# An adapter and expert FFN kernel on one core: Bx spread by hi/lo products, flips grouped, W's first piece halved, loads and transposes reordered

## The reference, cut to what matters

```python
Bx  = einsum('bni,bri->bnr', x, B[itok])          # x (8, 512, 2048), rank 16
y   = einsum('bnr,bor->bno', Bx, A[itok])
base   = einsum('bsi,oi->bso', y, base_w) + base_b            # base_w (2048, 2048)
hidden = einsum('bsi,ri->bsr', y, ffn_A)                      # rank 64
probs  = softmax(einsum('bsi,ei->bse', y, router_w))          # 16 experts, top 2, renormalised
delta  = einsum('bse,bsr,eor->bso', combine, hidden, ffn_B) * 0.5
out = x + base + delta
```

## Time and profile before

| | us |
|---|---|
| median of 3 runs | 446.18 (445.64 to 464.56) |
| the profiled execution's own time | 445.62 |
| its span, first to last instruction | 443.8 |
| granted TensorE clock, mean | 0.996 |

### The profile page before, as it was taken

How to read it: one execution, slowest core, us unless ns; L and a number is a source line. 1 busy time by engine, 2 the same in 40 slices (tenths; PEclk the granted TensorE clock), 3 DMA queues, 4 the chain that set the end, 5 groups by cost and what they waited for, 6 DMA issues and landing times.

```text
span 443.8 us, 6785 instructions
## 1 busy us (share of the span) xinstructions
PE 409.7 (92%) x2496; PEld 279.9 (63%) x2496; DVE 319.4 (72%) x830; ACT 108.1 (24%) x163; POOL 40.5 (9%) x53
## 2 busy tenths in 40 slices
PE   0597997999788999999999999999999999999996
PEld 0475985656556766666667666666666676666665
DVE  2699996999468496668677875966686778756453
ACT  0003114435473231123113112311231131123110
POOL 4020000002100120012001201200120012012000
PEclk9999998999999999999999999999999999999999
DMA  8999999999999999899999999998999898556935
GB/s 223 357 330 331 334 357 366 345 269 336 289 295 239 352 362 323 279 349 342 310 287 378 306 315 302 366 312 295 348 335 325 285 366 303 207 201 217 343 128 189
DMA packets 75027, 135.35 MB, mean 305 GB/s; under 512 B 5506, under 2 KB 14770, under 8 KB 74994
## 3 DMA queue, kind: packets, MB, share of 16 engines
q1 hardware_dynamic: 56000, 102.08, 69.7%
q10 hardware_dynamic: 18994, 32.84, 23.5%
HBM read 99.23 MB, written 35.65 MB: 304 GB/s over the span
## 4 chain that ended last, share of the span: by engine, by line
PE 63%; DVE 10%; DMA 9%; SPq 6%; POOL 3%; ACT 3%; issue 3%; ACTq 2%; POOLq 0%; DVEq 0%
PE ps L927 13%; PE ps L928 11%; PE ps L929 11%; PE ps L901 11%; PE ps L941 6%; DMA bexpT<-in_x 6%; PE ps L930 5%; POOL u_r L480 3%; DMA gm_r<-xT 3%; DVE xT L728 3%; DVE early L659 3%; SPq L296 3%; ACT bexpT L495 2%; PE ps L856 2%; PE ps L949 2%
## 5 line engine op out<-in xcount | busy, mean ns | idle before, releaser
L840 DVE TENSOR_TENSOR xbuf<-ps,xbuf 128x512 f32<-128x512 f32 x128 | 86.7, 677 | 96.0 <-PE ps L930 96.0
L927 PE MATMUL ps<-h_r,u_r 128*128 128x512 f32 x256 | 108.8, 425 | 0.7
L928 PE MATMUL ps<-h_r,u_r 128*128 128x512 f32 x256 | 100.3, 392 | 0.0
L929 PE MATMUL ps<-h_r,u_r 128*128 128x512 f32 x256 | 100.1, 391 | 0.0
L866 PE MATMUL ps<-early 128*128 128x256 f32 x256 | 66.5, 408 | 22.6 <-DVE early L659 22.6
L728 DVE STREAM_TRANSPOSE xT<-xbuf 128x256 f32<-128x256 f32 x224 | 80.6, 410 | 0.0
L866 PEld LDWEIGHTS ps<-early 128*128 128x128 f32 x256 | 48.1, 201 | 36.8 <-issue 16.5
L927 PEld LDWEIGHTS ps<-h_r,u_r 128*128 128x128 f32 x256 | 48.1, 188 | 35.9 <-issue 16.7
L659 DVE STREAM_TRANSPOSE early<-xbuf 128x256 f32<-128x256 f32 x128 | 65.9, 577 | 5.3 <-issue 3.8
L901 PE MATMUL ps<-bexpT,cur 128*32 128x512 f32 x512 | 61.6, 598 | 2.2 <-DVE h_r L707 1.5
L495 ACT ACTIVATE h_r<-ps 128x512 fp32r<-128x512 f32 x64 | 36.2, 595 | 78.8 <-PE ps L901 78.4
(11 more groups left out here) (67 smaller groups left out, 205.3 us busy)
## 6 DMA issues: line engine op xcount, KB each, us to landing
out<-xbuf SPq DMA_DIRECT2D x31, 1024.0 KB, 7.3
xbuf<-in_x SPq DMA_DIRECT2D x28, 1024.0 KB, 7.4
xbuf<-in_x ACTq DMA_DIRECT2D x32, 512.0 KB, 10.9
xbuf<-in_x SPq DMA_DIRECT2D x32, 512.0 KB, 8.6
xbuf<-in_L_ffn_base_w SPq DMA_DIRECT2D x16, 512.0 KB, 19.3
xbuf<-in_L_ffn_base_w ACTq DMA_DIRECT2D x16, 512.0 KB, 20.1
gm_r<-g_hilo SPq DMA_DIRECT2D x128, 32.0 KB, 6.8
early_u<-in_L_ffn_B SPq DMA_DIRECT2D x10, 256.0 KB, 18.5
```

What stands on the lines that cost most here:

```text
L840: dve.tensor_tensor(xs, ps[:, tile_bank(b.n, m), :], xs, ALU.add).then_inc(s_out, 1)
L927: pe.matmul(acc, u_r[:, b.q, 0, h, tok_t], hi, start=(h == 0), stop=False)
L928: pe.matmul(acc, u_r[:, b.q, 0, h, tok_t], lo, start=False, stop=False)
L929: pe.matmul(acc, u_r[:, b.q, 1, h, tok_t], hi, start=False, stop=False)
```

## The change

- Bx' is split: ACT makes a second copy of the PSUM bank rounded to fp32r (`bxs_r[:, 0]`), DVE subtracts it from `bxp` (`bxs_r[:, 1]`), and PE spreads both by two fp32r products into one sum, in slot 10 (`REP_AT`) instead of 9. ACT's `bx` and `sbx_r` copies move to slot 10 with it.
- Both halves' flips are done in slot 13 (`CT_AT`).
- Bx of batches 2 to 7 starts before tile 4 rather than 3; `T_AT` changes for these.
- W's first piece is loaded, transposed and multiplied in two halves of its columns.
- `cond_B` is loaded behind W's fourth piece; B's transposes at n = 46 (24 before), ffn_A's at 34 (36).
- Batch 0: x transposes at n = 88 to 106 (82 to 104), Bx after n = 94 and 104 (90 and 101), slots 8, 9, 10 at n = 105, 107, 110 (103, 106, 109).
- `dynamic_dma_scratch_size=1024` in the builder, which frees room for `bxs_r`.

```diff
-        X_AT = {82 + 3 * j // 2: j for j in range(KD)}
-        BX_AFTER = {90: 3, 101: 8}
-        SLOT_AT = {103: 8, 106: 9, 109: 10, 112: 11, 115: 12, 119: 13, 123: 14}
+        X_AT = {88 + 5 * j // 4: j for j in range(KD)}
+        BX_AFTER = {94: 4, 104: 8}
+        SLOT_AT = {105: 8, 107: 9, 110: 10, 112: 11, 115: 12, 119: 13, 123: 14}
-        BT_AT, FA_AT, GA_AT, SEL_AT = 24, 36, 56, 72
+        BT_AT, FA_AT, GA_AT, SEL_AT = 46, 34, 56, 72
+        WT = WN // SQ // 2
-        T_AT = {0: (5, 6), 1: (7,), 3: (8, 9), 4: (10, 11), 5: (12,), 6: (13, 14), 7: (15,)}
+        T_AT = {0: (5, 6), 1: (7,), 4: (8, 9), 5: (10, 11), 6: (12, 13), 7: (14, 15)}
-            return {4 if f.n == 1 else 3: range(0, KD), 8: range(KD, 2 * KD)}.get(m, ())
+            return {4: range(0, KD), 8: range(KD, 2 * KD)}.get(m, ())
-        CT_AT = UP_AT = {13: 0, 14: 1}
+        REP_AT, CT_AT = 10, 13
+        UP_AT = {13: 0, 14: 1}
+        def load_first_w(eng, qs):
+            for h in range(2):
+                for q in qs:
+                    eng.dma_start(w_in[0][q * SQ:(q + 1) * SQ, h * WT:(h + 1) * WT], w_q[0, q, :, h * WT:(h + 1) * WT])\
+                       .then_inc(s_w0[q // 2] if h == 0 else s_load[q // 2][0], 16)
...
             # ACT, slot 8
             copy(bxp, ps[:, BXB, :]).then_inc(s_bxp, 1)
+            need(act, s_rep, f.n)
+            copy(bxs_r[:, 0, :], ps[:, BXB, :]).then_inc(s_bxhi, 1)
...
             # DVE, w_transpose: indices below 16 take the second half only
+                if n < KD:
+                    wide = wT[:, n % RING, :].rearrange("p (h t l) -> p h t l", h=2, l=SQ)
+                    src = w_in[0][:, WT:2 * WT].rearrange("p t (l r) -> p r t l", l=SQ)[:, s]
+                    dve.transpose(wide[:, 1], src).then_inc(s_wt, 1)
+                    return
+            def first_transpose(s):
+                need(dve, s_wmm0, s - RING + 1)
+                dve.transpose(wide[:, 0], src).then_inc(s_wt0, 1)
...
             # DVE, slot 9, ahead of the maximum
+                    dve.wait_ge(s_bxp, f.n + 1)
+                    dve.wait_ge(s_bxhi, f.n + 1)
+                    dve.tensor_tensor(bxs_r[:, 1, :], bxp, f32(bxs_r[:, 0, :]), ALU.subtract).then_inc(s_bxlo, 1)
...
             # PE, slots
-                    pe.matmul(ps[:, BXB, :], spread[:, f.q, :], bxp,
-                              start=True, stop=True).then_inc(s_rep, 1)
+                if m == REP_AT:
+                    pe.wait_ge(s_bxhi, f.n + 1)
+                    pe.wait_ge(s_bxlo, f.n + 1)
+                    pe.matmul(ps[:, BXB, :], spread[:, f.q, :], bxs_r[:, 0, :], start=True, stop=False)
+                    pe.matmul(ps[:, BXB, :], spread[:, f.q, :], bxs_r[:, 1, :], start=False, stop=True)\
+                      .then_inc(s_rep, 1)
+                if m == CT_AT:
                     pe.wait_ge(s_combk, f.n * 2 + 2)
+                    for h in range(2):
+                        if h == 1:
+                            pe.wait_ge(s_bx, f.n + 1)
...
+            for s in range(KD):
+                first_product(s)     # PE; DVE runs first_transpose(s) likewise
```

More of the change, by code:

```diff
@@ L116, in adaln_ffn @@
         ident = sb("ident", [P, P])
-        spread = sb("spread", [P, 2, P])
+        spread = sb("spread", [P, 2, P], F32R)
+        bxs_r = sb("bxs_r", [P, 2, T], F32R)
         pick = sb("pick", [P, 2, RK])
@@ L163, in adaln_ffn @@
         s_load = [[sem(f"w_loaded{k}_half{h}") for k in range(WB)] for h in range(2)]
+        s_w0 = [sem(f"w_first_half{h}") for h in range(2)]
+        s_wt0, s_wmm0 = sem("w_first_transposed"), sem("w_first_used")
         s_ein = [sem(f"expert_in{k}") for k in range(7)]
@@ L357, in _ @@
             load_w(sp, 3, (0, 1))
+            load_cond_b(sp, (0, 1))
             load_experts(sp, 1, 0)
@@ L498, in _ @@
             load_cond_a(act, 1)
-            load_w(act, 0, (2, 3))
+            load_first_w(act, (2, 3))
             load_w(act, 1, (2, 3))
-            load_cond_b(act, (2, 3))
             load_w(act, 2, (2, 3))
@@ L506, in _ @@
             load_w(act, 3, (2, 3))
+            load_cond_b(act, (2, 3))
             load_experts(act, 1, 1)
@@ L515, in copy_experts @@
                 act.wait_ge(s_ef, g + 1)
-                for at, there, count in ((0, s_a, NB), (0, s_bT, KC), (1, s_fat, 2), (1, s_sm, 1),
-                                         (2, s_xe, 2 * KD)):
-                    if g == PER_C * at:
+                for first, there, count in ((0, s_a, NB), (2, s_bT, KC), (PER_C, s_fat, 2), (PER_C, s_sm, 1),
+                                            (2 * PER_C, s_xe, 2 * KD)):
+                    if g == first:
                         act.wait_ge(there, count)
@@ L655, in w_transpose @@
                 need(dve, s_wmm, n - RING + 1)
-                if n == 0:
-                    dve.wait_ge(s_const, 1)
+                if n < KD:
[3 more added lines that the diff above has]
+                    return
                 src = w_in[g % WB].rearrange("p t (l r) -> p r t l", l=SQ)[:, s]
                 dve.transpose(wT[:, n % RING, :].rearrange("p (t l) -> p t l", l=SQ), src).then_inc(s_wt, 1)
+            def first_transpose(s):
+                if s == 0:
+                    for half in range(2):
+                        dve.wait_ge(s_w0[half], NQ // 2 * 16)
+                    dve.wait_ge(s_const, 1)
+                need(dve, s_wmm0, s - RING + 1)
+                wide = wT[:, s % RING, :].rearrange("p (h t l) -> p h t l", h=2, l=SQ)
+                src = w_in[0][:, 0:WT].rearrange("p t (l r) -> p r t l", l=SQ)[:, s]
+                dve.transpose(wide[:, 0], src).then_inc(s_wt0, 1)
             def b_transposes():
@@ L797, in _ @@
             take_a()
+            for s in range(KD):
+                first_transpose(s)
             for n in range(NW):
@@ L860, in w_product @@
                 g, s = n // KD, n % KD
-                if n == 0:
-                    pe.wait_ge(s_a, NB)
+                if n < KD:
+                    pe.wait_ge(s_wt, n + 1)
+                    pe.matmul(ps[:, ACC, WN // 2:WN], a_t[:, s, :], wT[:, n % RING, WN // 2:WN],
+                              start=(s == 0), stop=(s == KD - 1)).then_inc(s_wmm, 1)
+                    return
                 if s == 0:
@@ L867, in w_product, with first_product @@
                           start=(s == 0), stop=(s == KD - 1)).then_inc(s_wmm, 1)
+            def first_product(s):
+                if s == 0:
+                    pe.wait_ge(s_a, NB)
+                pe.wait_ge(s_wt0, s + 1)
+                pe.matmul(ps[:, ACC, 0:WN // 2], a_t[:, s, :], wT[:, s % RING, 0:WN // 2],
+                          start=(s == 0), stop=(s == KD - 1)).then_inc(s_wmm0, 1)
             def expert_flips(g):
@@ L933, in bx_products @@
             def bx_products(f, m):
-                for k in bx_before(f, m):
+                for k in bx_before(m):
                     g, j = k // KD, k % KD
@@ L951, in slot @@
                     ins.then_inc(s_lg, 1)
-                    pe.matmul(ps[:, BXB, :], spread[:, f.q, :], bxp,
-                              start=True, stop=True).then_inc(s_rep, 1)
-                if m in CT_AT:
-                    h = CT_AT[m]
-                    pe.wait_ge(s_combk, f.n * 2 + 2)
[L957 to L962, removed]
+                if m == REP_AT:
+                    pe.wait_ge(s_bxhi, f.n + 1)
[4 more added lines that the diff above has]
+                if m == CT_AT:
+                    pe.wait_ge(s_combk, f.n * 2 + 2)
+                    for h in range(2):
+                        if h == 1:
+                            pe.wait_ge(s_bx, f.n + 1)
+                        for t in range(NT):
+                            w = combk[:, t, h * EH:(h + 1) * EH, :].rearrange("p e k -> p (e k)")
+                            ins = flip((MISC, BXB)[h], t * P, w)
+                        ins.then_inc(s_ct, 1)
             pe.wait_ge(s_masks, 4)
             first = Batch(0)
+            for s in range(KD):
+                first_product(s)
             for n in range(NW):
```

9 lines of the change are left out of this document (4 added, 5 removed).

## The result

| | before | after |
|---|---|---|
| median, us | 445.8 (6 runs, 444.65 to 464.56) | 451.57 (6 runs, 450.11 to 454.48) |
| ratio to before, 95% interval | | 1.0149 [1.011, 1.0187] |
| profiled execution: time, span | 445.62, 443.8 | 454.48, 452.6 |
| tile 0 of step 0 starts at | 116.32 | 123.05 |
| step 0; steps 1 to 5; step 6 | 50.0; 40.7; 40.5 | 49.6; 41.1; 40.9 |

The change makes the kernel 1.5% slower, which is under 2% but clear of no change: 5.8 us in the median, where 1.6 were forecast. Of the kernel before, the run of 464.56 was in a slower state of the chip and the ratio leaves it out. The profiled execution of the kernel after is the slowest of its six, so its ramp is an extreme.

What follows compares the result with a forecast made beforehand. The ramp was taken as a race between DVE's transposes and data arrival, the steps as bound by PE. Sum: 445.6 + 1.0 (ramp) - 0.3 (step 0) + 1.5 (six steps) = 447.8 us; range 441.5 to 451.5.

Steps and rivals of the forecast that it cites:

- the ramp: Up to about 116 us, before the steps: +1.0 us, bounds -2.8 and +3.
- the term for PE standing at the flips: Ramp: PE waits some 3 us for expert load 5 and 4.5 us for load 6.
- Bx behind flips 6: Ramp, batch 0: flips wait for load 6 until 81.0; DVE stops 1.3 us, starting pair 8 at 83.5.
- Behind pair 8: Ramp, after pair 8: subtraction adds 0.6 us, and DVE stops another 0.6 at slot 9.
- The clock: Ramp, after PE's load waits: a clock fall adds 2.2 us to flips and three products; ramp +1.6, without it -0.2.
- The start: Ramp's start: DVE begins 2.9 us sooner, half transposes lose 0.6; the early start is given back waiting for x.
- Bx before tile 4: Steps 1 to 6: 0.5 us saved behind h, but DVE's last transposes come late; net loss 0.5 to 0.6.
- The spread: Each step, 0 included: two fp32r products replace the fp32 spread, saving 0.3 us, extra copy and subtraction covered.
- Flips together in slot 13: Steps, behind tile 12: one format switch less, 0.1 us, gains nothing; zero, at worst 0.35.
- the scratch option: Builder option: nothing should depend on it, as no DMA is issued from POOL's program; 0.
- In time: Rival, steps: DVE delivers the last pairs before PE wants them, each step gains 0.5 + 0.3; 440.5 us, chance 0.2.
- Restart dearer: Rival, Bx's second half: pick-up after the wait costs 0.6 us instead of 0.1, ramp at +2; 451.8 us, chance 0.18.

Runs made afterwards that it cites:

- e2: Kernel after, with pairs 8 to 15 of x transposed four each in slots 4 and 5 for batches 2 to 7; 443.94 us, ratio 0.9958.
- e3: Kernel after, with Bx before tile 3 and the old order of x transposes for batches 2 to 7; 446.45 us, ratio 1.0025.
- e4: Kernel after, with the spread as one fp32 product in slot 9, without second copy and subtraction; 453.25 us, ratio 1.0192.
- e7: Kernel after, with 16 and 14 identity products added on PE before flips 5 and 6; 452.39 us, ratio 1.0161.
- e8: Kernel after, with W's first piece whole again; 450.51 us, ratio 1.0114.
- e1: Kernel after, with flips of experts 6 at n = 95 instead of 92; 452.4 us, ratio 1.0153.
- e5: Kernel after, with flips of experts 6 at n = 95 and 8 at n = 111, and e2's `T_AT`; 445.86 us.
- e9: Kernel after, with only flips of experts 6 moved to n = 95 and of experts 8 to n = 111; 451.13 us.
- e11: The kernel of e5 run again, unchanged; 442.84 us.
- e12: The kernel of e9 run again, unchanged; 450.32 us, ratio 1.0124.
- e6: Kernel after, with the old indices for batch 0's x, Bx and slots 8 to 10, and e2's `T_AT`; 441.18 us, ratio 0.9897.
- e13: Kernel after, with only the old indices for batch 0's x, Bx and slots 8 to 10; 449.28 us, ratio 1.0094.
- e14: The kernel of e6 run again, unchanged; 441.3 us, ratio 0.9889.
- e10: Kernel before, with the scratch option of the builder alone; 445.98 us.

## Why the prediction was wrong

The failed step is the ramp: the term for PE standing at the flips. The forecast had +1.0 us for the ramp; measured are 6.7 in the profile, and 3.7 is what the median leaves for it. The prediction named the first of the two places and the order of events there, but put the term too low, and it left out the second place. The kernel came out 3.8 us above the forecast (451.6 against 447.8); 2.7 of it are the ramp's, about 0.9 the steps'.

*Bx behind flips 6.* Forecast: load 6 landed at 81.0, DVE stopped for 1.3 us, and the low clock cost at most 2.2 more. In the profile it landed at 83.53 and the stop was 5.31; in e2, e3, e4, e7 and e8, which have the same order, the flips began at 81.0 to 81.9 and the stop was 1.97 to 4.19. I took the one landing time of the kernel before for a constant. SP issued the load 0.8 us later than before (63.6 for 62.8), and it was there 19.9 us later instead of 18.2. In the profile pair 8 came 5.6 us later than forecast without the clock's fall (89.14 against 83.5): 2.5 are the landing, 2.6 the clock, the rest the flips and products at full clock, which take 2.98 to pair 8. e1 shows that flips 6 are the cause of that stop. In the five other profiles the landing is near the forecast's, so a late landing of load 6 explains the profiled execution and not the median.

*What stands behind flips 8.* The prediction doesn't have it. Moving the logits from n = 106 to 107 put them behind flips that wait for experts 8. In the profile of the kernel after DVE is late anyway and nothing is seen of it. But in e3, e4 and e7, with flips 6 at their old place, the chain to tile 0 runs through the landing of load 8 (97.6 to 98.4), in e2 and e8 through that of load 6; and in e1 it costs 5.65. So two late loads set nearly the same time, and to free one of them gains little. With both free, tile 0 is at 114.3 to 116.2 in seven profiles (e5, e9, e11 and e12 by the flips, e6, e13 and e14 by the old indices). The price is 2.3 us by e13 and 2.8 by e6. The flips of 8 moved alone were not tried.

*Behind pair 8.* From there to tile 0 the forecast needs 32.6 us (116.1 - 83.5), measured are 33.91, in the kernel before 33.39. Part of it is a slip in the sum: by its own rows the stop before the subtraction was 2.6 + 1.1 - 2.5 = 1.2, not 0.6, and it measured 1.10. What made up the other 0.7 was not looked for.

*The clock.* The forecast weighed the rule of the Trainium skill, "TensorE: Matmul & The Clock Gate", section "HAM oscillation", that waits for data between bursts put the array back to its lower clock. The trace agrees: 0.57, 0.86, 0.50 and 0.79 in four windows behind the waits. The forecast's alternatives were 2.2 us or nothing; in the profile it cost 2.6 up to pair 8 and in e2, where flips 6 also took 1.97, 1.4 (4.42 against 2.98). Not all of it arrives at tile 0: e2 and e3 both have tile 0 at 119.27, though e3's pair 8 is 1.5 us earlier, because load 8 then holds e3. The same goes for e7. What part of the median is the clock's stays open.

*The start.* Right in what counted: DVE began at 12.63 (forecast 12.5) and waited 3.20 us for x until 71.53 (2.8, until 71.8), so the early start was given back there. One term was too small: the 32 halves took 4.73 + 4.61 us, 1.3 more than 16 whole transposes at 0.50, where I had put 0.6. It doesn't matter, as DVE waits for x afterwards in any case (e8).

*Bx before tile 4.* The mechanism was right: DVE needed 8.93 us from its add of tile 4 (225.91) to the end of the last transpose (234.84), with 8.9 forecast; and by the earlier trace rows tile 8's first product was to come 0.5 to 0.6 later than before. It came 0.8 later (235.44 - 213.78 = 21.66, before 20.85, both by PE's timeline). The 0.25 that are missing lie, as far as the rows tell, in the restart: tile 8 started 0.60 us after the last transpose ended. I had put 0.1 for the pick-up; the rival with the dearer restart had 0.6 and was nearer.

*The spread.* Right: 0.3 forecast, 0.36 by e3, 0.37 by e4, and 0.36 in step 0 (49.64 against 50.0). *Flips together in slot 13* and *the scratch option* (e10): nothing seen, as forecast. The step as a whole: forecast +0.25, measured +0.41, that is +0.8 for the move and -0.36 for the spread.

*The rivals.* "In time" (steps of 39.9) was wrong for this kernel, and it is what e2 reaches with the same transposes in another order. I rejected it rightly, by the sum of DVE's rows. "Restart dearer" had 451.8 us, the nearest to the result, in part by its mechanism (the restart, in steps of 41.1 where it had 41.4) and in part by luck, with a ramp worse than its +2.

What stays open: why e5 and e11 fall into the wait for reloads while e6 and e14, at the same pace, do not. In the windows from 285 to 366 us the former moved 305 to 315 GB/s with the engines full (1.06), the latter 329 to 332 at 0.97. And the medians of e9 and e12 lie 3 to 5 us above their profiled executions, which no trace explains. e11 had the wait with a ramp no earlier (116.23) than e6's (115.49), so an early ramp alone is not the reason.

## What to carry to other kernels

In the program of an engine that works in order, ask of each piece that is moved which waits it now stands behind, and give a load's landing a spread of some microseconds, not the one value of a trace: products with their data ready were held here by flips that waited 3.37 us. When two queues feed each other, place what the consumer needs next ahead of what nobody waits for yet; e2 took 1.19 us a step, 7.1 in six steps, by putting eight transposes before two adds. And where removing one stop, or one cause of it, doesn't change the time, look in the chain of waits for the stop that it hid (e1, e7) before the theory is dropped.

## What the runs showed of the hardware

The granted clock fell to 0.50 (1.2 GHz) from 84 to 88 us, after PE had been waiting 4.43 us and 3.37 us with eight flips and some products between; eight flips then took 1.97 us where 1.09 is their time at 1.00. Thirty short products in the waits (e7) kept it at 1.00. The same order with other landings gave other clocks: flips 5 ran at full rate in e5 behind a wait of 3.40 us (1.09) and at half rate in e4 behind one of 3.52 (1.97).

From the end of DVE's last transpose to the first product behind Bx it took 0.60 us in the step, and 0.61 in the ramp before, though what follows is fp32r in the one and fp32 in the other. The last Bx products, fp32 in both, are in it.

From 285 to 366 us the DMA engines read full (1.06) at 305 to 315 GB/s in two executions (e5, e11) and moved 329 to 332 at 0.96 to 0.97 in two others (e6, e14), with the same work in a step. So the engines' share alone doesn't tell the rate. "DMA: Bandwidth & Descriptors" of the Trainium skill, section "Where 436 GB/s comes from", puts the limit of memory at about 358 GB/s for a core, half of what two cores share. One core runs here, and the trace goes above that figure: slices of 11.3 us of the kernel after reach 380 GB/s, reads and writes together, with 299 in the mean of the span.
